# Slot steps of a graph kernel: rows of indices fetched by DMA, and a step's work dealt anew to ScalarE and GpSimd

## What is computed

```python
m_j = einsum('bnd,do->bno', h, W1[:D]);  m_i = einsum('bnd,do->bno', h, W1[D:])
pre = m_j[:, None, :, :] + m_i[:, :, None, :] + b1
msg = gelu(layernorm(pre, g1, be1))
agg = einsum('bijo,bij->bio', msg, adj)
out = layernorm(concat([h, agg], -1) @ W2 + b2, g2, be2)
```

## Time and profile before

| | |
|---|---|
| time before, median of 3 runs | 4111.16 us (4110.72 to 4120.36) |
| profiled execution, its own time | 4122.07 us |
| its span, first to last instruction | 4120.2 us |
| busy: PE, DVE, ACT, POOL | 3577.9, 3411.6, 2808.7, 2154.7 us |
| mean granted TensorE clock | 0.923 of full |
| moved by DMA | 73.95 MB, 18 GB/s on average |

### The profile page before, as it was taken

How to read it: one execution, slowest core, us unless ns; L and a number is a source line. 1 busy time by engine, 2 the same in 40 slices (tenths; PEclk the granted TensorE clock), 3 DMA queues, 4 the chain that set the end, 5 groups by cost and what they waited for, 6 DMA issues and landing times.

```text
span 4120.2 us, 103754 instructions
## 1 busy us (share of the span) xinstructions
PE 3577.9 (87%) x30351; PEld 3064.0 (74%) x30772; DVE 3411.6 (83%) x12271; ACT 2808.7 (68%) x6445; POOL 2154.7 (52%) x1987
## 2 busy tenths in 40 slices
PE   3494789889899999989899898998999898998998
PEld 2283778778787787868778786877878687786887
DVE  4788888898888888888888888888888888887840
ACT  2484776858667685866858686685858668595753
POOL 1182763719456382844728274572828447292730
PEclk7596889999998999989999898989989899999999
DMA  2000001000010100001010000101000010000000
GB/s 80 26 1 26 1 1 42 1 25 17 1 42 1 42 0 21 21 1 42 1 42 0 21 22 1 42 1 42 0 21 21 1 42 1 26 0 1 16 1 21
DMA packets 95517, 73.95 MB, mean 18 GB/s; under 512 B 7504, under 2 KB 95184, under 8 KB 95184
## 3 DMA queue, kind: packets, MB, share of 16 engines
q1 hardware_dynamic: 95184, 70.09, 5.6%
HBM read 61.68 MB, written 8.39 MB: 17 GB/s over the span
## 4 chain that ended last, share of the span: by engine, by line
PE 61%; DVE 16%; ACT 8%; issue 8%; POOL 3%; DVEq 2%; ACTq 0%; POOLq 0%; DMA 0%; SPq 0%
PE n_bank_d L1512 11%; PE n_bank_c L1501 9%; PE n_bank_b L1501 9%; PE n_bank_c L1598 9%; PE n_bank_d L1615 4%; PE n_bank_d L1616 4%; PE n_bank_d L1612 3%; PE n_bank_a L1484 3%; PE n_bank_b L1676 2%; DVE v_normed L987 1%; DVE v_normed L1149 1%; POOL v_z L517 1%; PE n_bank_a L1472 1%; DVE v_z L1109 1%; ACT v_pair L858 1%
## 5 line engine op out<-in xcount | busy, mean ns | idle before, releaser
L517 POOL TENSOR_TENSOR v_z<-v_z,all_bc_L_gnn_be 128x512 f32<-128x512 f32 x620 | 788.3, 1273 | 32.4 <-DVE v_z L1109 32.4
L1512 PE MATMUL n_bank_d<-v_diag,v_msg 128*128 128x128 f32 x4960 | 618.3, 278 | 25.1 <-ACT v_diag L756 25.1
L531 POOL TENSOR_TENSOR v_prstd<-v_pvar,all_neg_half 128x8 f32<-128x8 f32 x310 | 561.8, 1812 | 105.7 <-DVE v_pvar L1125 76.9
L1512 PEld LDWEIGHTS n_bank_d<-v_diag,v_msg 128*128 128x128 f32 x4960 | 577.0, 192 | 28.1 <-ACT v_diag L756 28.1
L756 ACT ACTIVATE v_diag<-all_ident,v_value 128x128 f32<-128x128 f32 x1860 | 573.6, 389 | 0.0
L1501 PEld LDWEIGHTS n_bank_b<-v_parts,v_onehot 128*128 128x128 bf16 x8208 | 473.4, 98 | 90.6 <-ACT n_bank_b L688 56.9
L1501 PE MATMUL n_bank_b<-v_parts,v_onehot 128*128 128x128 bf16 x8208 | 512.8, 219 | 26.2 <-ACT n_bank_b L688 26.1
L1501 PEld LDWEIGHTS n_bank_c<-v_parts,v_onehot 128*128 128x128 bf16 x7440 | 442.0, 100 | 108.9 <-ACT n_bank_c L688 64.6
L1501 PE MATMUL n_bank_c<-v_parts,v_onehot 128*128 128x128 bf16 x7440 | 479.8, 222 | 42.1 <-ACT n_bank_c L688 42.1
L1598 PE MATMUL n_bank_c<-all_l_wsd,v_fT 128*128 128x256 f32 x1792 | 457.8, 398 | 28.4 <-ACT v_adjT L673 25.9
L683 ACT ACTIVATE v_fT<-n_bank_d,all_l_c 128x256 f32<-128x256 f32 x256 | 120.0, 475 | 461.0 <-PE n_bank_d L1616 460.8
(11 more groups left out here) (283 smaller groups left out, 7435.5 us busy)
## 6 DMA issues: line engine op xcount, KB each, us to landing
v_adj_l<-in_adj SPq DMA_DIRECT2D x128, 256.0 KB, 3.6
v_adj_x<-in_adj SPq DMA_DIRECT2D x64, 256.0 KB, 3.5
v_ring<-in_x SPq DMA_DIRECT2D x16, 512.0 KB, 6.0
out_x<-v_xout SPq DMA_DIRECT2D x64, 128.0 KB, 1.9
w_wu<-in_L_gnn_wu SPq DMA_DIRECT2D x4, 192.0 KB, 2.5
all_W<-in_L_gnn_W SPq DMA_DIRECT2D x2, 128.0 KB, 4.0
w_raw<-in_L_gnn_ws SPq DMA_DIRECT2D x1, 192.0 KB, 3.0
w_raw<-in_L_gnn_wd SPq DMA_DIRECT2D x1, 192.0 KB, 3.2
```

The source lines that it names most:

```text
L517: nc.gpsimd.tensor_tensor(z[par][:, units], z[par][:, units], wide(bc["L2_gnn_be1"])[:, units], ALU.add).then_inc(sem["z_ready"], 1)
L531: nc.gpsimd.tensor_tensor(prstd[:], pvar[:], minus_half, ALU.pow).then_inc(sem["prstd_ready"], 1)
L1512: ins = nc.tensor.matmul(ps_agg[:, u // NB, (u % NB) * P:(u % NB + 1) * P], msg[par][:, u], diag[par][:, u], start=False, stop=False, skip ...
```

## The change

- The spread leaves PE and ACT. `indexT` is one chunk in SBUF; SP stores each chunk to an internal DRAM table `slot_rows`, waits until it has landed, and then fetches one row at a time, by a DMA that reads the 2 KB row for each of the 128 partitions (256 KB a slot), into one of two `spread` buffers. The rows of slots 0 and 1 are fetched in `mix`, ahead of SP's layer-0 loads. Every later row is fetched in a new `slots` part of SP's program that comes after the whole of its `mix`: row s once `pick` of slot s-1 is done.
- `pick` waits for its DMA in place of ACT's copy. PE's `spread_out` and ACT's `keep_spread` go.
- POOL's two diagonals go; ACT makes all eight.
- ACT's order in a step becomes: seed of half 0, gelu of half 1, seed of half 1, gelu of half 0, eight diagonals.

```diff
+            def spread_out(slot, par):
+                sp.dma_start(spread[:, par], slot_rows[bass.ds(slot, 1)].broadcast_to((P, UNITS * P)))\
+                    .then_inc(spread_in[par], 16)
+
+            def first_spreads(a, again):
+                sp.wait_ge(sem["slots_ready"], a + 1)
...
+                with sp.Fori(0, chunks) as c:
+                    sp.wait_ge(sem["index_kept"], first + c + 2)
+                    sp.sem_inc(keep["held"], 1)
+                    sp.dma_start(slot_rows[bass.ds(c * P, P)], indexT[:]).then_inc(index_stored, 16)
+                sp.reg_add(stored, stored, chunks)
+                sp.wait_ge(index_stored, sp.snap(stored) * 16 + 16)
+                sp.sem_inc(keep["held"], 1)
...
+                for par in range(2):
+                    spread_out(par, par)
+
+            def slots(a):
+                pairs = sp.snap(n_pairs)
+                before = sp.snap(sp.snap(count) + a * 2)
+                with sp.Fori(1, pairs + 1) as i:
+                    for par in range(2):
+                        sp.wait_ge(sem["onehot_ready"], before + (i * 2 + par))
+                        sp.sem_inc(keep["held"], 1)
+                        spread_out(i * 2 + par, par)
...
                     load_extract(g + 2)
+                if l1:
+                    first_spreads(g + 1, again)
...
             with sp.Fori(1, GROUPS - 3) as g:
                 mix(g)
+                slots(g + 1)
...
                     if not first:
                         shift(1 - par, step, 1)
-                        diagonals(1 - par, step, slot - 1)
...
                 def diagonals(par, steps, slot):
                     act.wait_ge(sem["summed"], steps * 2 + 2)
-                    for u in range(BY_ACT):
+                    for u in range(UNITS):
...
-                def act_step(par, step, slot, first=False, second=False):
-                    ahead = act.snap(step + g * 2 + 2)
-                    act.wait_ge(sem["onehot_ready"], ahead)
-                    keep_spread(g, ahead)
-                    if not (first or second):
+                def act_step(par, step, slot, second=False):
+                    act.wait_ge(sem["z_made"], step * 2 + 1)
+                    seed(1 - par, 0)
+                    if not second:
                         gelu(par, act.snap(step - 1), 1)
-                    if not first:
-                        for half_ in range(2):
-                            act.wait_ge(sem["z_made"], step * 2 + (half_ + 1))
-                            seed(1 - par, half_)
-                        gelu(1 - par, step, 0)
-                        diagonals(1 - par, step, slot - 1)
-
-                act_step(0, before, 0, first=True)
+                    act.wait_ge(sem["z_made"], step * 2 + 2)
+                    seed(1 - par, 1)
+                    gelu(1 - par, step, 0)
+                    diagonals(1 - par, step, slot - 1)
...
             def pick(ahead, par):
-                dve.wait_ge(sem["spread_kept"], ahead + 1)
+                dve.wait_ge(spread_in[par], (ahead + (2 - par)) * 8)
...
                     gather(1 - par, pe.snap(step + g + 1), 0)
-                    pe.wait_ge(sem["spread_kept"], ahead + 1)
-                    spread_out(slot + 3)
                     gather(1 - par, pe.snap(step + g + 1), 1)
...
-                pe.wait_ge(sem["spread_kept"], first_ahead + 1)
-                spread_out(1)
```

More of the change, by code:

```diff
@@ L212 @@
 HALF = UNITS // 2
-BY_ACT = 6
 LOWEST = -3.4028235e38
@@ L268, in network @@
         node_of = plan.sb("node_of", [P, NB])
-        spread = plan.sb("spread", [P, UNITS * P], BF16)
+        spread = plan.sb("spread", [P, 2, UNITS * P], BF16)
         junk = plan.sb("junk", [P, 2, N], BF16)
@@ L366, in network @@
         x_in = s.sem("x_in")
+        index_stored = s.sem("index_stored")
+        spread_in = [s.sem(f"spread_in{i}") for i in range(2)]
         adj_in = [s.sem(f"adj_in{b}") for b in range(GB)]
@@ L518, in shift, with pool_step @@
                                             ALU.add).then_inc(sem["z_ready"], 1)
[L520 to L527, removed]
+                def pool_step(par, step, first=False):
                     if not first:
@@ L533, in pool_step @@
                         shift(1 - par, step, 1)
-                        diagonals(1 - par, step, slot - 1)
-                pool_step(0, before, 0, first=True)
-                pool_step(1, pool.snap(before + 1), 1)
+                pool_step(0, before, first=True)
+                pool_step(1, pool.snap(before + 1))
                 with pool.Fori(1, pairs) as i:
                     for par in range(2):
-                        slot = pool.snap(i * 2 + par)
-                        pool_step(par, pool.snap(before + slot), slot)
+                        pool_step(par, pool.snap(before + (i * 2 + par)))
                 pool.reg_add(count, count, pairs * 2)
@@ L545, in slots @@
                 shift(1, after, 1)
-                diagonals(1, after, pool.snap(pairs * 2 - 1))
             def mix(g, l1=True, l0=True, l3=True, u=True):
@@ L688, in seed @@
                 nc.scalar.activation(ps_m[par][:, units], own[:, units], ACT.Copy).then_inc(sem["seeded"], 1)
-            def keep_spread(g, ahead):
-                act.wait_ge(sem["spread_made"], ahead + (g + 1))
-                nc.scalar.activation(spread[:], ps_spread, ACT.Copy).then_inc(sem["spread_kept"], 1)
             def load_slots(a):
@@ L703, in keep_index @@
                     act.wait_ge(sem["index_turned"], first + c + 1)
-                    nc.scalar.activation(indexT[:, bass.ds(c, 1)].rearrange("p a n -> p (a n)"), ps_index,
-                                         ACT.Copy).then_inc(sem["index_kept"], 1)
+                    act.wait_ge(index_stored, (first + c) * 16 + 16)
+                    nc.scalar.activation(indexT[:], ps_index, ACT.Copy).then_inc(sem["index_kept"], 1)
                 act.reg_add(kept, kept, chunks)
             def start_slots(g, before):
-                first_ahead = act.snap(before + g * 2)
                 for i in range(2):
@@ L1480, in layer0_out @@
                 ins.then_inc(sem["out_made"], 1)
-            def spread_out(slot):
-                for c in range(2):
-                    ins = nc.tensor.matmul(bank_a[:, c], ident16[:, bass.ds(slot % P, 1)].broadcast_to((P, P)),
-                                           indexT[:, bass.ds(slot // P, 1), c * 512:(c + 1) * 512].rearrange("p a n -> p (a n)"),
-                                           start=True, stop=True)
-                ins.then_inc(sem["spread_made"], 1)
             def slots(g):
```

55 lines of the change are left out of this document (28 added, 27 removed).

## The result

The changed kernel takes 4125.0 us, median of 12 runs (4114.0 to 4128.6); the kernel before took 4117.0 in 12 runs beside it. The ratio is 1.0018, 95% interval 1.0011 to 1.0026: 8 us slower, inside the 0.3% that the prediction called no change. The profiled execution has a span of 4126.8 us; that of before had 4120.2. It is such a small difference of large terms that the total says little: the parts have to be measured.

A forecast was written before the change was run, and what follows sets the result against it. The prediction took POOL's full ring to bound the step at 5.12 us. 4122.1 - 42 + 70 + 6 - 11 - 5 = 4140, +18 on the profiled execution, which lies 10.9 above the median, so 4129 us; range 4080 to 4180.

The forecast's parts named there:

- The bound: Steady step before the change: POOL is full and sets 5.12 us, and PE reaches the same length by waiting.
- POOL's ring: Closed loop of POOL's power, two shifts and diagonals with DVE's variance, claimed to set the old step at 5.12 us.
- DVE's ring: Loop of variance, power, two normalises and statistics, 4.93 us with the short variance, claimed longest after the change.
- The steady step: Distance between variances inside a group: 245 distances shrink from 5.117 to 4.945 us on average, -42 us.
- rival (b): Steady step stays at 5.12 us, the variance being long of itself or another engine closing a ring: 4171 us; chance 0.14.
- The row's landing: DMA of a row in a steady step: 2.7 us, with issue 3.1, leaving 1.0 us to spare.
- Rival (c): A row lands later than 3.7 us in every step: at 4.2, +140 us, 4270; chance 0.08.
- The first pick: Start of 14 groups: the pick of slot 2 waits for a row queued behind refill loads, +70 us, bounds 33 and 95.
- Rival (a): The first row of a group slips past the loads or lands early, costing 33 us: 4086 us, faster; chance 0.16.
- The clock: PE's granted clock falls to 0.50 after idling in all 14 waiting groups: +6 us, up to +30, or 0.
- Rival (d): PE's low clock lasts into several steps: 4153 us or more; chance 0.10.
- Ends and mix: Last variance to last aggregate shortens, -11 us over 16 groups; slot 1's spread leaves PE's path in mix, -5 us.

The follow-up runs named there:

- the kernel with the later row: Against the changed kernel with slots 2 and 3 fetched ahead of the refill loads: each row issued only after the next power; 4016.6 us, ratio 0.9742.
- the kernel with two queues: Against the changed kernel: ACT issues the refill loads on its own DMA queue, SP the first row after step 0's variance; 4154.4 us, ratio 1.0085.
- the kernel with rows 2 and 3 first: Against the changed kernel: SP fetches the row of slot 2 before the output stores and that of slot 3 before the refill loads; 4042.7 us, ratio 0.9825.
- the copies: Three useless variance operations between variance and pick, added to the kernel with rows 2 and 3 first: 4025.1 us; added to the kernel before: 4104.1 us.

## Why the prediction was right, and where it was off

**The bound.** Right in the main: POOL's ring with the long variance held the step at 5.12, and DVE's ring holds it now; the kernel without POOL's diagonals and the one that puts them back show it from both sides. The reading that PE "has come to the same length by waiting" holds for the last 0.11 us alone: freed of POOL, PE with its spread still takes 5.01.

**The steady step**, forecast 4.94 and -42 us. Measured -47.7, the lines "fourth" and "all later ones" of the table together. The later ones are 230 distances: 5.118 us on average before, 4.917 after (4.93 in most groups, 4.83 in the first), 0.20 less each where the prediction had 0.17. (It took off 49 early distances; 16 groups have 48.) The reading of the variance's two durations was right; rival (b) is out.

**The row's landing**, forecast 2.7 us and with issue 3.1. Measured:

```profile
DMA to landing us min/median/max: 3.0/3.1/5.4
```

It is 3.1 us after its issue, 0.4 more than the load in the earlier trace rows, and the pick had its row in all steady steps. The spare of 1.0 was 0.7; counted to where DVE waits anyhow it is 1.3, as the kernel with the later row shows. Rival (c) is out.

**The first pick**, forecast +70. Measured +72.6. So close a sum is in part luck, for two of its terms were off and cancelled. The prediction had the row issued 0.15 us ahead of the moment at which the pick wants it and landing 5.8 us later. Over the twelve groups the row was issued 1.4 us after the variance, because the variance comes earlier beside SP's loads than in the earlier trace rows, and landed 4.8 us after its issue. The wait was 6.07 us on average (6.97 in the place shown) and not 5.65; it lengthened the first distance by 5.5, where the prediction had 5.35. Over the run the picks waited 80.6 us. The last two groups have first distances of 7.9 and 8.1, some 3 us more than a step, as said. The reason was right in part. In all twelve groups the row landed 0.64 us behind the ring load, so the order in one ring, for which the prediction cites the Trainium skill, agrees with the trace. But the kernel with two queues shows that the loads' bytes delay the row from another queue as well: its place in the ring was not what made it late. Rival (a), which hoped that the row slips past, is out.

**The clock**, forecast +6. This is the term that was mis-sized: second and third distances together, +13.9 and -18.0, it was about -4. The prediction took over the slow third steps of the earlier trace rows and added one for every group that waits. None of the 16 groups has a slow third step any more: it is 4.93 us (4.83 in the first group), at the full clock. In the kernel before it was slow (6.4 to 6.7) in 10 groups, 9 of them among the 14 that wait now; the prediction counted 11 and 10. Some 3 us of the -18.0 are the shorter step itself. Instead the granted clock is down in the second distance of all 16 groups, 0.59 to 0.82 on average over it, and costs 1.2 us in nine of them (6.12 against 4.93) and 0.3 to 0.8 in the others. The waits make this worse but are not its cause alone: in the first two groups, whose picks do not wait, PE idles 2.1 and 2.0 us in the first distance, the clock over the second is 0.68, and it takes 5.26 and 5.29; and in the kernel with rows 2 and 3 first, 11 groups show the same. PE's idle 2.63 us before the third step's gather, for a seed of ACT's, is gone with the change. Its lower bound for the term, 0, was not low enough. Rival (d), a low clock over several steps, is out: it is over by the third.

**Ends and mix**, forecast -11 and -5. Measured -17.8 + 3.5 = -14.3, but it is a right sum of two wrong terms. From the last variance to the end of the last aggregate the 16 groups took 166.6 us before and 167.5 after, +0.9 and not -11: at the full clock this is 10.09 us against 10.38, 0.3 less and not 0.7, and in five groups, with a granted clock of 0.57 to 0.69 over its last part, it is 10.5 to 11.7. The other -15 lie in the rest of the stretches. They are not shown to come from the spread of slot 1, which the prediction named: the kernel before without POOL's diagonals keeps that spread, and its stretches between groups are 20.2 us shorter all the same.

**The sum** was to be +18; by the terms it is +6.5, 11.5 less. The clock made 10 of that and the shorter step 6; the first pick and the ends made 4 the other way. The direction of the forecast, slower, was right; but the 0.63 that it gave to slower by over 0.3% was too much for a net of two large terms: it came out at 0.18%, inside the range to which it gave 0.20. That the forecast time, 4129, lies only 4 us from the measured 4125.0 is luck besides: the kernel before took 4117.0 us beside it and not 4111.2, which hid 6 of the 10 us by which the difference was off (8 against 18).

What the prediction did not see at all is that the power's 1.82 in the earlier trace rows holds 0.16 of another engine's work. It took a duration from a row and used it as the price of the operation.

## What to carry to other kernels

When work is moved to DMA, its first transfer of a stage competes with whatever loads are issued there: put the one that is needed at once ahead of the bulk in time; a queue of its own did nothing for it here, while the bytes of the other queue were under way. A duration in a trace is a price plus what ran beside it: compare the same instruction's minimum and median before taking it as fixed, above all for GpSimd beside DVE. When one bound is lifted, look for the next one just below it: here PE stood 0.11 us under POOL. And before the clock loss of an idle stretch is taken over into the sum, look whether the change leaves that stretch where it was.

## What the runs showed of the hardware

A GpSimd power over 128x8 took 1.65 us, and 1.81 (1.93 at most) if a VectorE comparison over 128x1024 in bf16 was already running; the comparison took 0.88 us beside the power in either order, and 1.90 where it met GpSimd's addition over 128x512. So the power does not hinder the comparison, though it runs beside the whole of it, and the addition does so for 1.0 of its own 1.27 us. A lock for the whole instruction, as the section of the Trainium skill named above has it, would have made a comparison that begins 0.05 us behind the power wait for its end; here the measurement decides, and it did not wait.

A row of 2 KB read by 128 partitions, 256 KB in all, landed after 3.1 us (the median) when alone, 4.4 to 5.4 us after its issue behind 1.5 MB in its own queue, and 5.1 to 7.2 us with the 1.5 MB in another queue. The first group's steps are 0.1 us shorter than all others, 4.83 against 4.93, and 4.66 against 4.76 with the copies; why was not followed.
